# First steps of a fused token-embedding, scan and expert kernel: the taps' load and scaling moved ahead of the embedding's, the first one-hot matrix built in halves, and ten products of zeros added on TensorE

## The chip, the cores and the metric

The kernel runs on 1 core of one Trainium2 chip. The metric is the device time of one execution in microseconds (us). Before the change it was 185.24 us, the median of three runs that gave 185.24, 184.29 and 185.25. One more execution was recorded by the hardware profiler; all durations below are from that one.

## The reference

Three layers on 8 sequences of 512 token numbers, with 128 channels. Only the first is touched by the change.

```
# token layer; fake_quant(w) = round(w / s) * s, with s = max|w| / 127
e   = fake_quant(emb_weight)[x]               # 125 x 128 table, one row per token
h   = relu(e[t-1] * w[0] + e[t] * w[1])       # w = fake_quant(conv_weight), per channel, e[-1] = 0
# scan layer
u   = layernorm(h)
X_t = A X_{t-1} + B u_t                       # 4 heads of 64, each state divided by its largest entry
h   = h + (e^2 X / max|X|) C + u D
# expert layer
n   = layernorm(h); a = layernorm(n)*g + b; a = a W_attn^T + b_attn + n
h   = h + gelu((gelu(a F1_e^T + b1_e) F2_e^T + b2_e) W_next^T + b_next)
```

## The kernel before

Each of the five engines has a program of its own, written out in order by hand; semaphores join them. A batch b (0 to 7) is one sequence. Its 512 tokens are laid out so that 16 steps of 32 chunks stand side by side.

**The table.** The embedding (125x128) and the two taps (1x256, tile conv_w) are quantised on the chip. VectorE takes the largest magnitude of every row of the embedding (L634, amax_e). TensorE transposes that column against the identity matrix, which lies in the packed constants pc (L1037), so that VectorE can take the maximum over all rows (L645) and from it the scale, its inverse and the rounded table (L646 to L648). The taps are scaled in a chain of five instructions on one partition (L637 to L641): maximum, scale, reciprocal, multiply and add the rounding constant, take the constant off again. The function `chained` makes the next instruction of the engine wait for the one before it. A product with a row of ones (L1041) copies the taps to all partitions, into bank 7. Then VectorE multiplies table and taps (L653, L655), takes the combined scale scale_h (L657), and splits the products in two bf16 halves (L658); tab_ready is the semaphore behind it.

**The lookup.** It is a product with a one-hot matrix. `spread_ids(b)` (L938) copies the token numbers of batch b to 125 partitions of bank b % 2; it needs the numbers as bf16 (ids_b) and a bf16 identity (ident_b), which GpSimd casts (L413, L415) once pc and the numbers have landed. `one_hot(b)` compares them with the partition's number, 512 columns (L665) and then 31 columns (L668), the chunk before. `gather(b)` (L949) makes 16 products of 128 columns into bank 2, four for each quarter q. It waits for the one-hot matrix and, from b = 1, for bank 2 to be free. ScalarE applies scale and ReLU (L521, h).

**The loop around it.** For each batch VectorE builds the one-hot matrix two batches ahead, takes the statistics of h (L673, L677), and normalises its part of u (L697); GpSimd computes the reciprocal root (L426 to L429); ScalarE copies h, then normalises the rest of u (L538), which stands in its program ahead of the next batch's h; TensorE transposes u (L960), and in the gaps multiplies powers of A (L901) and, from batch 6, state inputs (L973). TensorE's order is fixed: `gather(b)`, `spread_ids(b + 2)`, powers, `transpose_u(b - 2)`, powers. Before the loop TensorE waits for the packed array pa and the copy pw of a part of it.

**The queues.** SyncE asks for emb_w, ids_i, pa, pw, pb, and the two expert weights, in that order. ScalarE's queue asks for pc and then conv_w. GpSimd starts with four fills (ones1, neg_half, ids_b, one column of onehot), each of which raises pool_const; ScalarE waits for the first of them ahead of a small activation that loads its table.

Behind this stage come the scan's carries, and a long stage of mixing, attention and expert products that starts at about 50 us. The change edits none of it.

Of the kernel before, what the change touches and what calls it, by code (L numbers as in the profile page):

```python
# [95 lines left out]
def build(nc, ids, emb, conv, pack_a, pack_b, pack_c, fc1, fc2, out):  # L96
    with ExitStack() as ctx:
# [3 lines left out]
        def sem(name):  # L101
            return ctx.enter_context(nc.semaphore(name))
# [64 lines left out]
        with ExitStack() as early:  # L167
            def sb_early(name, shape, dt=F32):
                return early.enter_context(nc.sbuf_tensor(name, shape, dt))


            fc2_w = sb_early("fc2_w", [P, NE * HID])
            fc1_w = sb_early("fc1_w", [P, NE * HID])
            ids_i = sb_early("ids_i", [NB, L], I32)
            ids_b = sb_early("ids_b", [P, L], BF16)
            ident_b = sb_early("ident_b", [P, P], BF16)
            centre = sb_early("centre", [P, P])
            attn_g = sb_early("attn_g", [P, CH])
        hid_p = [sb(f"hid_p{s}", [P, 2, HC, HALF], F32R) for s in range(NS)]
# [10 lines left out]
        ld_ids, ld_emb, ld_pa, ld_pb = sem("ld_ids"), sem("ld_emb"), sem("ld_pa"), sem("ld_pb")  # L190
        ld_pc, ld_fc1, ld_fc2 = sem("ld_pc"), sem("ld_fc1"), sem("ld_fc2")
        v2_ready, ld_conv = sem("v2_ready"), sem("ld_conv")
        pool_const = sem("pool_const")
        pool_link, dve_link = sem("pool_link"), sem("dve_link")
        ids_ready, amax_e_ready, tab_ready = sem("ids_ready"), sem("amax_e_ready"), sem("tab_ready")
        attn_g_ready, taps_ready = sem("attn_g_ready"), sem("taps_ready")
# [174 lines left out]
        with nc.Block() as block:  # L371

            @block.sync
            def _(sp):
                sp.dma_start(emb_w[:], emb).then_inc(ld_emb, 16)
                sp.dma_start(ids_i[:], ids).then_inc(ld_ids, 16)
                sp.dma_start(pa[:], pack_a).then_inc(ld_pa, 16)
                sp.dma_start(pw[:, 0, :], pack_a[:, PA["a"]]).then_inc(ld_pa, 16)
                sp.dma_start(pb[:], pack_b).then_inc(ld_pb, 16)
                sp.dma_start(fc2_w[:].rearrange("p (e m) -> p e m", e=NE), fc2).then_inc(ld_fc2, 16)  # L380
                sp.dma_start(fc1_w[:], fc1).then_inc(ld_fc1, 16)
                for b in range(NB - 1):

                    if b < NB - 2:
                        sp.wait_ge(res_ready, b + 1)
                    else:
                        sp.wait_ge(late_res_ready, 1)
                    sp.dma_start(out[b], res[:, b % 2, :]).then_inc(stored[b % 2], 16)
                for half in range(2):

                    b, s = NB - 1, slice(half * HALF, (half + 1) * HALF)
                    sp.wait_ge(last_res_ready, half + 1)
                    sp.dma_start(out[b][:, s], res[:, b % 2, s]).then_inc(stored[b % 2], 16)
                sp.wait_ge(stored[0], 16 * (NB // 2))
                sp.wait_ge(stored[1], 16 * (NB // 2 + 1))

            @block.gpsimd
            def _(pool):
                nc.gpsimd.memset(ones1[:], 1.0).then_inc(pool_const, 1)
                nc.gpsimd.memset(neg_half[:], -0.5).then_inc(pool_const, 1)  # L400
                nc.gpsimd.memset(ids_b[:], 0.0).then_inc(pool_const, 1)
# [76 lines left out]

            @block.scalar
            def _(act):  # L480
                act.dma_start(pc[:], pack_c).then_inc(ld_pc, 16)
                act.dma_start(conv_w[:], conv).then_inc(ld_conv, 16)
                act.wait_ge(pool_const, 1)

                nc.scalar.activation(warm[:], ones1[0:1, 0:1], ACT.Gelu)
# [30 lines left out]
                for b in range(NB + 2):  # L516
                    if b < NB:
                        act.wait_ge(gat_done, b + 1)
                        if b == 0:
                            act.wait_ge(tab_ready, 1)  # L520
                        nc.scalar.activation(h[:, b, :], bank[2][:], ACT.Relu, scale=scale_h[:]).then_inc(h_ready, 1)  # L521
                    for t in prep_tasks(b, 0):
                        copy_out_prep(t)
                    if b >= 2:
                        act.wait_ge(u_t_done, b - 1)
                        nc.scalar.activation(uT[:, b - 2, :, :].rearrange("p i k -> p (i k)"), bank[3][:],
                                             ACT.Copy).then_inc(uT_ready, 1)
                    for t in prep_tasks(b, 1):
                        copy_out_prep(t)
                    if 1 <= b <= NB and U_DVE[b - 1] < NQ:  # L530
                        act.wait_ge(rstd1_ready, b)
                        if b == 1:
                            act.wait_ge(h_ready, 1)
                        if b >= 3:
                            act.wait_ge(u_t_done, b - 2)
                        for q in range(U_DVE[b - 1], NQ):
                            s = slice(q * CH, (q + 1) * CH)
                            last = nc.scalar.activation(u[:, (b - 1) % 2, s], h[:, b - 1, s], ACT.Identity,  # L538
                                                        scale=rstd1[:, b - 1, q:q + 1], bias=shift1[:, b - 1, q:q + 1])
                        last.then_inc(u_act_ready, 1)  # L540
                    if b in (NB - 2, NB - 1):
                        copy_runs(0, b - (NB - 2))
                    if b >= NB:
                        copy_fused(b - NB)
# [78 lines left out]
            def _(dve):  # L623
                link = [0]

                def chained(ins):

                    link[0] += 1
                    ins.then_inc(dve_link, 1)
                    dve.wait_ge(dve_link, link[0])  # L630


                dve.wait_ge(ld_emb, 16)
                nc.vector.tensor_reduce(amax_e[:], emb_w[:], AX.X, ALU.max,  # L634
                                        apply_absolute_value=True).then_inc(amax_e_ready, 1)
                dve.wait_ge(ld_conv, 16)
                chained(nc.vector.tensor_reduce(amax_c[:], conv_w[:], AX.X, ALU.max, apply_absolute_value=True))  # L637
                chained(nc.vector.tensor_scalar(taps[:, 2 * CH:], amax_c[:], 1.0 / QMAX, None, ALU.mult))
                chained(nc.vector.reciprocal(inv_c[:], taps[:, 2 * CH:]))
                chained(nc.vector.tensor_scalar(taps[:, 0:2 * CH], conv_w[:], inv_c[:], ROUND, ALU.mult, ALU.add))  # L640
                nc.vector.tensor_scalar(taps[:, 0:2 * CH], taps[:, 0:2 * CH], -ROUND, None,  # L641
                                        ALU.add).then_inc(taps_ready, 1)

# [10 lines left out]
                                               op0=ALU.add, op1=ALU.mult)  # L654
                chained(nc.vector.scalar_tensor_tensor(out=tab[:, 0], in0=both, scalar=-ROUND, in1=q_taps,  # L655
                                                       op0=ALU.add, op1=ALU.mult))
                nc.vector.tensor_tensor(scale_h[:], scale_e[:], bank[7][:, 2 * CH:2 * CH + 1], ALU.mult)  # L657
                nc.vector.tensor_tensor(tab[:, 1], prod[:], tab[:, 0], ALU.subtract).then_inc(tab_ready, 1)  # L658

                def one_hot(b):  # L660
                    dve.wait_ge(idb_done, b + 1)
                    if b >= 2:
                        dve.wait_ge(gat_done, b - 1)
                    src = bank[b % 2][0:VOC, :]
                    nc.vector.tensor_scalar(onehot[:, b % 2, NCH:], src, float(VOC - 1), pc[0:VOC, PC["iota"]],  # L665
                                            ALU.min, ALU.is_equal)

                    nc.vector.tensor_scalar(onehot[:, b % 2, 1:NCH], src[:, L - NCH:L - 1], float(VOC - 1),  # L668
                                            pc[0:VOC, PC["iota"]], ALU.min, ALU.is_equal).then_inc(oh_ready, 1)

                def statistics(b, st, st_ready, mv, mv_ready):
                    for q in range(NQ):
# [4 lines left out]
                        last = nc.vector.bn_aggr(mv[:, b, q, :], st[:, b % 2, q, :])  # L677
                    last.then_inc(mv_ready, 1)

                dve.wait_ge(ld_pc, 16)  # L680
                dve.wait_ge(pool_const, 4)
                one_hot(0)
                one_hot(1)
                for b in range(NB + 1):
                    if b + 2 < NB:
                        one_hot(b + 2)
# [203 lines left out]
            def _(pe):  # L890
# [44 lines left out]
                def spread_ids(b):  # L935
                    if b >= 2:
                        pe.wait_ge(oh_ready, b - 1)
                    mm(bank[b % 2][0:VOC, :], ident_b[:, b:b + 1].broadcast_to([P, VOC]), ids_b[:], start=True,  # L938
                       stop=True).then_inc(idb_done, 1)

                def gather(b):
                    pe.wait_ge(oh_ready, b + 1)
                    if b >= 1:
                        pe.wait_ge(h_ready, b)
                    for q in range(NQ):
                        for n, (tap, part) in enumerate([(0, 0), (0, 1), (1, 0), (1, 1)]):

                            at = (q * TQ + tap) * NCH
                            last = mm(bank[2][:, q * CH:(q + 1) * CH], onehot[:, b % 2, at:at + P], tab[:, part, tap, :],  # L949
                                      start=(n == 0), stop=(n == 3))  # L950
                    last.then_inc(gat_done, 1)
# [80 lines left out]
                    mm(scan_bank(a), a1, every_run(g, a, q), start=False, stop=True).then_inc(state_done[g], 1)  # L1032


                pe.wait_ge(ld_pc, 16)
                pe.wait_ge(amax_e_ready, 1)
                nc.tensor.transpose(bank[6][:, 0:VOC], amax_e[:].broadcast_to([VOC, P]),  # L1037
# [4 lines left out]
                pe.wait_ge(ids_ready, 2)  # L1042
                spread_ids(0)
                spread_ids(1)
                pe.wait_ge(ld_pa, 32)
                for b in range(NB + 2):
                    if b == 0:
# [228 lines left out]
```

## Time and profile before

| | |
|---|---|
| runs | 185.24, 184.29, 185.25 us |
| profiled execution | 185.18 us, span 183.4 us |
| TensorE matmuls | 166.1 us busy, 91% of the span |
| VectorE | 131.8 us, 72% |
| ScalarE | 95.0 us, 52% |
| GpSimd | 92.8 us, 51% |
| mean granted TensorE clock | 0.997 |

The span is from the first to the last instruction of the trace. A row of the timeline has start, duration, engine, line, operation, tile written and tiles read, and in brackets the idle time of the engine just before it with what ended it; rows marked x16 are 16 instructions put together, with the time from the first start to the last end. PEld is the weight load of TensorE. Names with q (SPq, ACTq) are DMA issues. Line numbers such as L949 are those of the code.

### The profile page before, as it was taken

The numbers are of one execution on the slowest core, as the hardware profiler recorded it, in microseconds if no ns is written. First come the engines' busy times: TensorE is split into PE (matmuls) and PEld (weight loads), VectorE is DVE, ScalarE is ACT, GpSimd is POOL, SyncE is SP. The second block draws the span as 40 slices with busy tenths as digits, with TensorE's granted clock in tenths as the row PEclk, the third lists the DMA queues.
The fourth block names the chain that finished last, engine by engine and source line by source line (L and its number), as shares of the span: only waits on it lengthen the run. The fifth ranks groups of instructions, "written<-read, shape, count | busy, mean of one in ns | idle before, by whom it ended". The sixth has DMA issues, their size and how long they took to land.

```text
span 183.4 us, 3366 instructions
## 1 busy us (share of the span) xinstructions
PE 166.1 (91%) x1123; PEld 134.7 (73%) x1123; DVE 131.8 (72%) x405; ACT 95.0 (52%) x220; POOL 92.8 (51%) x152
## 2 busy tenths in 40 slices
PE   0599899999999898988998999999999999998993
PEld 0187685687764367865765999999998999996992
DVE  1868984494531277579996599988888898629983
ACT  3027993443223222021335683977949687686692
POOL 3107665399930000040040496695978959688700
PEclk9999999999999999999999999999999999999998
DMA  4994000000000000000000000000010100101013
GB/s 146 359 422 211 2 4 0 2 2 4 0 0 0 0 4 0 0 0 2 4 0 0 0 0 4 0 33 30 0 57 2 61 0 4 57 2 59 13 47 114
DMA packets 2325, 7.53 MB, mean 41 GB/s; under 512 B 254, under 2 KB 892, under 8 KB 2052
## 3 DMA queue, kind: packets, MB, share of 16 engines
q1 hardware_dynamic: 2162, 7.18, 10.1%
q8 instruction: 9, 0.15, 0.3%
q10 hardware_dynamic: 146, 0.13, 0.2%
q14 instruction: 8, 0.07, 0.1%
HBM read 5.22 MB, written 2.10 MB: 40 GB/s over the span
## 4 chain that ended last, share of the span: by engine, by line
PE 52%; DVE 16%; POOL 11%; issue 9%; ACT 8%; DMA 2%; POOLq 0%; DVEq 0%; ACTq 0%
PE bank L1159 7%; POOL hid_p L448 6%; PE bank L973 6%; PE bank L1026 5%; PE bank L1179 5%; PE bank L1032 5%; PE bank L1105 4%; PE bank L949 3%; PE bank L926 3%; DVE u L697 3%; PE bank L1125 2%; PE bank L1102 2%; ACT gel L572 2%; PE bank L997 2%; DVE st L673 2%
## 5 line engine op out<-in xcount | busy, mean ns | idle before, releaser
L448 POOL TENSOR_TENSOR hid_p<-hid_f,hid_p 128x256 fp32r<-128x256 f32 x52 | 37.5, 741 | 21.2 <-ACT hid_p L596 19.6
L594 ACT ACTIVATE hid_f<-bank,pa 128x256 f32<-128x256 f32 x64 | 30.9, 486 | 12.9 <-PE bank L1159 12.7
L1159 PE MATMUL bank<-xaT_p,fc_p 128*128 128x256 f32 x192 | 35.3, 295 | 1.8 <-issue 0.8
L1179 PE MATMUL bank<-hid_p,out_hi 128*128 128x256 f32 x128 | 32.2, 287 | 0.2
L467 POOL TENSOR_TENSOR rstd<-spread,neg_half 128x8 f32<-128x8 f32 x8 | 13.2, 1648 | 37.5 <-DVE spread L831 37.5
L1159 PEld LDWEIGHTS bank<-xaT_p,fc_p 128*128 128x128 f32 x192 | 26.6, 188 | 5.3 <-issue 2.1
L1179 PEld LDWEIGHTS bank<-hid_p,out_hi 128*128 128x128 f32 x128 | 23.3, 188 | 1.0 <-POOL hid_p L448 0.9
L596 ACT ACTIVATE hid_p<-bank,pa 128x256 fp32r<-128x256 f32 x48 | 23.6, 491 | 0.0
L1105 PE MATMUL bank<-pb,xh 128*128 128x128 f32 x128 | 19.5, 275 | 0.0
L512 ACT ACTIVATE X<-bank 128x512 f32<-128x512 f32 x12 | 7.2, 598 | 21.4 <-PE bank L1032 21.4
L1179 PE MATMUL bank<-hid_p,out_lo 128*128 128x256 f32 x64 | 17.8, 279 | 0.0
L673 DVE BATCH_NORM_STATS2 st<-h 128x6 f32<-128x128 f32 x64 | 13.9, 280 | 4.5 <-ACT h L521 4.2
L1105 PEld LDWEIGHTS bank<-pb,xh 128*128 128x128 f32 x128 | 16.9, 192 | 0.0
L799 DVE TRANSPOSE_TENSOR_REDUCE amax<-X 128x16 f32<-128x512 f32 x16 | 10.4, 685 | 7.4 <-ACT X L512 7.4
L780 DVE SCALAR_TENSOR_TENSOR bank<-h,ratio,bank 128x128 f32<-128x128 f32 x32 | 9.0, 350 | 5.4 <-issue 5.1
L1102 PE MATMUL bank<-pb,uT 128*128 128x128 f32 x64 | 12.5, 276 | 0.5 <-DVE xh L855 0.5
L973 PE MATMUL bank<-uT,late_b 128*128 128x512 f32 x24 | 11.6, 600 | 0.7 <-ACT X L512 0.7
L1026 PE MATMUL bank<-uT,pa 128*128 128x512 f32 x24 | 12.2, 596 | 0.0
L1032 PE MATMUL bank<-X,pa 128*128 128x512 f32 x24 | 12.1, 592 | 0.0
L1179 PEld LDWEIGHTS bank<-hid_p,out_lo 128*128 128x128 f32 x64 | 12.0, 188 | 0.0
L812 DVE SCALAR_TENSOR_TENSOR xaT_p<-bank,attn_c,xaT_p 128x256 fp32r<-128x256 f32 x16 | 7.0, 478 | 6.9 <-ACT xaT_p L610 6.9
L949 PEld LDWEIGHTS bank<-tab,onehot 125*128 125x128 bf16 x128 | 9.2, 110 | 3.7 <-issue 3.5
(127 smaller groups left out, 339.5 us busy)
## 6 DMA issues: line engine op xcount, KB each, us to landing
fc_w<-in_fc SPq DMA_DIRECT2D x2, 2048.0 KB, 12.5
out<-res SPq DMA_DIRECT2D x7, 256.0 KB, 2.0
pa<-in_pack_a SPq DMA_DIRECT2D x1, 407.0 KB, 3.4
pb<-in_pack_b SPq DMA_DIRECT2D x1, 320.0 KB, 5.8
out<-res SPq DMA_DIRECT2D x2, 128.0 KB, 1.7
pc<-in_pack_c ACTq DMA_DIRECT2D x1, 128.5 KB, 2.9
pw<-in_pack_a SPq DMA_DIRECT2D x1, 64.0 KB, 5.5
emb_w<-in_emb SPq DMA_DIRECT2D x1, 62.5 KB
```

The source lines that it names most:

```text
L448: nc.gpsimd.tensor_tensor(hid_p[1][:, half, c, :], hid_f[:, m % HID_SLOTS, :], hid_p[0][:, half, c, :].bitcast(F32), ALU.subtract).then_in ...
L594: full = nc.scalar.activation(hid_f[:, m % HID_SLOTS, :], src, ACT.Gelu, bias=bias)
L596: nc.scalar.activation(hid_p[0][:, half, c, :], src, ACT.Gelu, bias=bias).then_inc(hid_ready, 1)
L673: last = nc.vector.bn_stats(st[:, b % 2, q, :], h[:, b, q * CH:(q + 1) * CH])
L949: last = mm(bank[2][:, q * CH:(q + 1) * CH], onehot[:, b % 2, at:at + P], tab[:, part, tap, :], start=(n == 0), stop=(n == 3))
L973: last = mm(scan_bank(a), b_then(a, RUN - 1 - q), u_runs(g, q), start=(q == 0), stop=(q == RUN - 1))
L1026: mm(scan_bank(a), b_then(a, 0), u_runs(g, q), start=True, stop=False)
L1032: mm(scan_bank(a), a1, every_run(g, a, q), start=False, stop=True).then_inc(state_done[g], 1)
L1102: mm(dst, uT[:, b, q * TQ:(q + 1) * TQ, :].rearrange("p i k -> p (i k)"), pb[:, PB["d"]], start=True, stop=False)
L1105: last = mm(dst, xh[:, b % 2, a, q * P:(q + 1) * P], pb[:, PB["c"]][:, a * CH:(a + 1) * CH], start=False, stop=(a == NP - 1))
L1159: last = mm(bank[5 + n % 2][:, 0:HALF], fc1_p[w][:, e * HID + c * P:e * HID + (c + 1) * P], xaT_p[m][:, b % 2, half, :], start=(k == 0), s ...
L1179: last = mm(out_bank(b, half)[:, half * HALF:(half + 1) * HALF], out_p[w][:, e, c * CH:(c + 1) * CH], hid_p[m][:, half, c, :], start=(c == ...
```

## The change

Five edits, all in the first steps:

1. ScalarE's queue asks for conv_w first, then for pc. VectorE waits for conv_w and runs the first four instructions of the taps' chain before it waits for the embedding; the fifth comes behind the embedding's row maxima.
2. `one_hot` makes the 31 columns first; for batch 0 the 512 columns are made in two instructions of 256, and the first raises the new semaphore oh_first. `gather(0)` starts at oh_first and waits for the rest ahead of its third quarter.
3. scale_h is computed behind `one_hot(0)`, with a semaphore of its own, scale_h_ready, for which ScalarE waits in place of tab_ready.
4. GpSimd fills a new tile zeros (128x512 bf16) ahead of its other fills.
5. TensorE multiplies zeros into bank 5: six products of 512 columns before its first real instruction, and four between `spread_ids(1)` and the loop. Nothing reads the results.

```diff
@@ gpsimd
+                nc.gpsimd.memset(zeros[:], 0.0).then_inc(zeros_ready, 1)
                 nc.gpsimd.memset(ones1[:], 1.0).then_inc(pool_const, 1)
@@ scalar
+                act.dma_start(conv_w[:], conv).then_inc(ld_conv, 16)
                 act.dma_start(pc[:], pack_c).then_inc(ld_pc, 16)
-                act.dma_start(conv_w[:], conv).then_inc(ld_conv, 16)
...
                         if b == 0:
-                            act.wait_ge(tab_ready, 1)
+                            act.wait_ge(scale_h_ready, 1)
@@ vector
-                dve.wait_ge(ld_emb, 16)
-                nc.vector.tensor_reduce(amax_e[:], emb_w[:], AX.X, ALU.max,
-                                        apply_absolute_value=True).then_inc(amax_e_ready, 1)
                 dve.wait_ge(ld_conv, 16)
                 chained(nc.vector.tensor_reduce(amax_c[:], conv_w[:], AX.X, ALU.max, apply_absolute_value=True))
                 chained(nc.vector.tensor_scalar(taps[:, 2 * CH:], amax_c[:], 1.0 / QMAX, None, ALU.mult))
                 chained(nc.vector.reciprocal(inv_c[:], taps[:, 2 * CH:]))
                 chained(nc.vector.tensor_scalar(taps[:, 0:2 * CH], conv_w[:], inv_c[:], ROUND, ALU.mult, ALU.add))
+                dve.wait_ge(ld_emb, 16)
+                nc.vector.tensor_reduce(amax_e[:], emb_w[:], AX.X, ALU.max,
+                                        apply_absolute_value=True).then_inc(amax_e_ready, 1)
                 nc.vector.tensor_scalar(taps[:, 0:2 * CH], taps[:, 0:2 * CH], -ROUND, None,
                                         ALU.add).then_inc(taps_ready, 1)
...
-                nc.vector.tensor_tensor(scale_h[:], scale_e[:], bank[7][:, 2 * CH:2 * CH + 1], ALU.mult)
...
                     src = bank[b % 2][0:VOC, :]
-                    nc.vector.tensor_scalar(onehot[:, b % 2, NCH:], src, float(VOC - 1), pc[0:VOC, PC["iota"]],
+                    number = pc[0:VOC, PC["iota"]]
+                    nc.vector.tensor_scalar(onehot[:, b % 2, 1:NCH], src[:, L - NCH:L - 1], float(VOC - 1), number,
                                             ALU.min, ALU.is_equal)
-                    nc.vector.tensor_scalar(onehot[:, b % 2, 1:NCH], src[:, L - NCH:L - 1], float(VOC - 1),
-                                            pc[0:VOC, PC["iota"]], ALU.min, ALU.is_equal).then_inc(oh_ready, 1)
+                    for n0, n1 in ((0, HALF), (HALF, L)) if b == 0 else ((0, L),):
+                        last = nc.vector.tensor_scalar(onehot[:, b % 2, NCH + n0:NCH + n1], src[:, n0:n1],
+                                                       float(VOC - 1), number, ALU.min, ALU.is_equal)
+                        if n1 < L:
+                            last.then_inc(oh_first, 1)
+                    last.then_inc(oh_ready, 1)
+                dve.wait_ge(ld_pc, 16)
+                dve.wait_ge(pool_const, 4)
+                one_hot(0)
+                nc.vector.tensor_tensor(scale_h[:], scale_e[:], bank[7][:, 2 * CH:2 * CH + 1],
+                                        ALU.mult).then_inc(scale_h_ready, 1)
+                one_hot(1)
@@ tensor
                 def gather(b):
-                    pe.wait_ge(oh_ready, b + 1)
-                    if b >= 1:
+                    if b == 0:
+                        pe.wait_ge(oh_first, 1)
+                    else:
+                        pe.wait_ge(oh_ready, b + 1)
                         pe.wait_ge(h_ready, b)
                     for q in range(NQ):
+                        if b == 0 and q == NQ // 2:
+                            pe.wait_ge(oh_ready, 1)
...
+                def keep_clock(n):
+                    for _ in range(n):
+                        mm(bank[5][:], zeros[:, 0:P], zeros[:], start=True, stop=True)
+                pe.wait_ge(zeros_ready, 1)
+                keep_clock(6)
                 pe.wait_ge(ld_pc, 16)
                 pe.wait_ge(amax_e_ready, 1)
...
                 spread_ids(0)
                 spread_ids(1)
+                keep_clock(4)
                 pe.wait_ge(ld_pa, 32)
```

## Rows read from the trace of the kernel before

**Rows 1.** Busy time in 20 to 25 us: PE, PEld, DVE, ACT, POOL, clock, DMA.
```profile
20.00:25.00 5.00, 4.89 (x51) 3.99 (x50) 4.92 (x25) 4.91 (x13) 3.32 (x9) 1.00 0.01 3
```

**Rows 2.** The chain that ended last, 0 to 60 us: start, duration, what.
```profile
0.73 3.10 DMA emb_w<-in_emb
...
7.81 0.07 DVE scale_h L657
...
8.31 0.66 DVE onehot L665
8.97 0.17 DVE onehot L668
...
36.91 3.90 DVE u L697 x4
```

**Rows 3.** The timeline, 0.7 to 4.3 us.
```profile
0.73 0.39 ACTq L481 DMA_DIRECT2D pc<-in_pack_c  x1
...
0.90 0.52 POOL L401 MEMSET ids_b<- 128x512 bf16 x1
1.15 0.55 ACTq L482 DMA_DIRECT2D conv_w<-in_conv  x1
...
3.78 0.29 POOL L413 CAST ident_b<-pc 128x128 bf16<-128x128 f32 x1 [2.32 <-DMA pc<-in_pack_c]
3.85 0.29 DVE L634 TENSOR_REDUCE amax_e<-emb_w 125x1 f32<-125x128 f32 x1 [3.85 <-DMA emb_w<-in_emb]
...
4.10 0.41 DVE L637 TENSOR_REDUCE amax_c<-conv_w 1x1 f32<-1x256 f32 x1
```

**Rows 4.** DMA issues: KB each, and median us from issue to landing.
```profile
out<-res SPq DMA_DIRECT2D x2, 128.0 KB, 1.7
pc<-in_pack_c ACTq DMA_DIRECT2D x1, 128.5 KB, 2.9
pw<-in_pack_a SPq DMA_DIRECT2D x1, 64.0 KB, 5.5
```

**Rows 5.** The timeline, 4.2 to 7.5 us.
```profile
4.28 0.44 PE L1037 MATMUL bank<-pc,amax_e 125*128 125x125 f32 x1 [4.28 <-DVE amax_e L634]
...
5.28 0.28 DVE L641 TENSOR_SCALAR taps<-taps 1x256 f32<-1x256 f32 x1
5.49 0.27 DVE L645 TENSOR_REDUCE amax_all<-bank 128x1 f32<-128x125 f32 x1
...
5.71 1.19 PE L1041 MATMUL bank<-taps,ones 1*128 1x257 f32 x2 [0.98 <-DVE taps L641]
...
6.83 1.12 PE L938 MATMUL bank<-ids_b,ident_b 128*125 128x512 bf16 x2
7.02 0.42 DVE L653 SCALAR_TENSOR_TENSOR prod<-rounded,bank 125x256 f32<-125x256 f32 x1 [0.56 <-PE bank L1041]
```

**Rows 6.** The timeline, 9.2 to 18.6 us.
```profile
9.28 1.86 PE L949 MATMUL bank<-tab,onehot 125*128 125x128 bf16 x16 [1.33 <-DVE onehot L668]
...
11.61 0.75 DVE L665 TENSOR_SCALAR onehot<-bank,pc 125x512 bf16<-125x512 f32 x1 [1.66 <-PE bank L938]
...
12.06 1.86 PE L949 MATMUL bank<-tab,onehot 125*128 125x128 bf16 x16
...
13.33 0.38 DVE L677 BATCH_NORM_AGGREGATE mv<-st 128x2 f32<-128x6 f32 x4
...
14.39 0.75 DVE L665 TENSOR_SCALAR onehot<-bank,pc 125x512 bf16<-125x512 f32 x1 [0.69 <-PE bank L938]
...
14.80 1.22 PE L949 MATMUL bank<-tab,onehot 125*128 125x128 bf16 x16
...
15.79 0.88 ACT L538 ACTIVATE u<-h,shift,rstd 128x128 f32<-128x128 f32 x2 [0.70 <-POOL shift L429]
...
17.53 1.06 PE L949 MATMUL bank<-tab,onehot 125*128 125x128 bf16 x16
```

**Rows 7.** Busy time in 10 to 11 us, same columns; the clock is the third from the right.
```profile
10.00:11.00 1.00, 1.00 (x12) 1.00 (x11) 0.00 (x0) 0.00 (x0) 0.00 (x0) 1.00 0.96 410
```

More of the change, by code:

```diff
@@ L176, in build @@
             ident_b = sb_early("ident_b", [P, P], BF16)
+            zeros = sb_early("zeros", [P, L], BF16)
             centre = sb_early("centre", [P, P])
@@ L192, in build @@
         v2_ready, ld_conv = sem("v2_ready"), sem("ld_conv")
-        pool_const = sem("pool_const")
+        pool_const, zeros_ready = sem("pool_const"), sem("zeros_ready")
+        oh_first, scale_h_ready = sem("oh_first"), sem("scale_h_ready")
         pool_link, dve_link = sem("pool_link"), sem("dve_link")
@@ L678, in statistics @@
                     last.then_inc(mv_ready, 1)
[L680 to L683, printed above, removed]
                 for b in range(NB + 1):
```

## The prediction

> **What bounds the kernel now.** I read the page's first part, then the chain of waits, then the timeline of the first 20 us. TensorE is busy 91% of the span, but in the first 9 us it mostly waits: the chain begins with the embedding's load, which lands 3.1 us after its issue [rows 2], goes through VectorE's quantising, over TensorE's copy of the taps, and back to VectorE [rows 5], and reaches `gather(0)` at 9.28 us. From there to 14.39 it is on TensorE: VectorE's one-hot matrix for batch 2 is kept waiting 1.66 us, that for batch 3 another 0.69 us, both for `spread_ids` behind a gather [rows 6]. From 14.39 VectorE has a job ready at nearly each moment for some 10 us (4.92 of 5.00 us in 20 to 25, with ScalarE at 4.91 and TensorE at 4.89 beside it [rows 1]), and everything behind depends on that chain. So the reader is to watch one number: when the one-hot matrix of batch 3 starts (14.39). What is gained up to there shifts the rest.
>
> **The clock.** 16 products of a gather take 1.86 us at 9.28 and at 12.06, 1.22 us at 14.80, and 1.06 us at 17.53 [rows 6]. 15 spacings of 128 columns account for the difference: about 0.107 us each early, 0.056 us late, which are 1.2 and 2.4 GHz. The column of the granted clock says 1.00 even at 10 us [rows 7]; I go by the durations. In the gather at 14.80 some 12 of 16 are already fast ((1.86 - 1.22) / 0.051), so the clock rose near 15.2 us. TensorE had then worked without a break since 9.28, for 5.9 us; before that it had stood still for 1.33 us.
>
> **Part by part.** The sum is made against the profiled execution (185.18 us; span 183.4, 1.78 around it), which is 0.06 below the median shown (185.24).
>
> *Taps first.* conv_w is issued at 0.73 instead of 1.15. Its landing isn't in the trace; the nearest rows are 1.7 us from issue (a 128 KB store) and 2.9 us (pc) [rows 4], so it lands between 2.43 and 3.63 (that it had landed by 4.10 excludes nothing here). I take 3.0. The first four instructions of the chain need 1.14 us (about 4.14 to 5.28, [rows 3, 5]), to 4.17, past the embedding's landing at 3.85, and the row maxima 0.29: call their end R = 4.46, against 4.14 before [rows 3]; the ends of the range are 4.14 and 5.06. So this edit first costs 0.32.
>
> It gives back more. Before, the first product with real use of R was VectorE's maximum at 5.49, held by the taps' chain, and prod at 7.02, held by the copy of the taps: R + 2.88. After, the transpose starts at R + 0.14, L1041 follows at R + 0.56, takes 1.19, and prod starts 0.12 behind it, at R + 1.87 = 6.33. VectorE's own way there, from the transposed maxima (R + 0.66) through four chained steps (0.98, 5.49 to 6.47), ends at R + 1.64 and fits beside it. Net 0.69.
>
> A sentence apart: the Trainium skill, "DMA: Bandwidth & Descriptors" (Anatomy of one DMA), puts the fixed part of a DMA on the GpSimd path at about 2.0 us; if ScalarE's queue did the same, R would be near 4.16 and prod near 6.0. No row shows the landing of so small a load.
>
> *pc later.* Its issue moves from 0.73 to about 1.28 (behind 0.55 of issue). With 2.9 us it lands at 4.2. The transpose needs it at R + 0.14 = 4.6, so 0.4 covers it; GpSimd's two casts (0.29 and 0.61, the first from 3.78) then end at 5.1, ahead of `spread_ids(0)` at 6.1. If pc lands later than 4.6, each 0.1 costs 0.1. The fill of zeros (0.52, the same shape as ids_b in [rows 3]) moves the other fills by about 0.45; ScalarE is busy with issuing until 1.7 and pays nothing.
>
> *One-hot in halves, scale_h later.* From prod (7.02 [rows 5]) to the first one-hot in the chain (8.31 [rows 2]) it was 1.29, less 0.07 for scale_h: 6.33 + 1.22 = 7.55. The 31 columns cost 0.17, the half 0.40 (on the line through 0.66 for 512 columns and 0.17 for 31 [rows 2]), a semaphore 0.14 (9.14 to 9.28): oh_first frees the gather at 8.26, against 9.28. VectorE has one more instruction, 0.14 more in all; it stands before `one_hot(1)`, which then ends at about 9.4 instead of 9.95, and isn't waited for. ScalarE's wait for scale_h (8.6) ends before the gather does.
>
> *Zeros.* Six products of 512 columns at 1.2 GHz are 6 x 0.427 = 2.56 us (512 at the spacing of the slow gather rows), from 1.3 to 3.9: before R, free. The four are in the way: TensorE reaches them at R + 0.56 + 1.12 + 0.86 = 7.0 (5.71 to 6.83, two spreads) and at 1.2 GHz leaves them at 8.7, 0.45 past oh_first. So `gather(0)` starts at 8.7 and not at 8.26: 0.58 gained of 1.02. What they buy is that TensorE works without a break from about 4.6.
>
> *What the clock does.* Unbroken work for 5.9 us went before the rise; from 4.6 that gives 10.5, and with the burst from 1.3 counted whole 7.2. I take 9.0. Then three gather products are slow and 13 fast; the gather ends at 9.9, its `spread_ids(2)` lands at 10.1, and VectorE starts batch 2 at 10.15 (11.61 before), ends its one-hot matrix, statistics and averages at 12.2 (2.06 us: 11.61 to 13.71 without a gap), and goes straight on to batch 3, whose `spread_ids(3)` is there by 12.0: `gather(1)` starts at 10.75 behind h(0) and takes 1.06. 14.39 - 12.2 = 2.2 gained. With a rise at 10.5 the same walk gives 1.4, with 7.2 it gives 2.8.
>
> *What is late next.* ScalarE's h(2) stands behind u(0), which waits for GpSimd's root: the averages ended at 13.71, u(0) started at 15.79 [rows 6], 2.08 later, and takes 0.88. Counted from 12.2 this makes h(2) start at 15.1, and the statistics of batch 2 at 15.8 (17.71 before): 0.3 of the 2.2 is lost there, though h(3), which goes by batch 1, keeps 2.2. The four instructions of u at 36.91 that take 3.90 instead of about 1.1 [rows 2] run beside GpSimd's cast of fc1, which starts on the same event; I let that stay as it is. Sum: 1.9 us, 185.2 - 1.9 = **183.3 us**; by the bounds of the rise and of R, 182.5 to 184.0.
>
> **The rivals.**
>
> *Products of zeros don't raise the clock.* Nothing in the trace shows a product of zeros. Then TensorE works without break only from 8.7, the clock rises at about 14.6, and the gain is `gather(0)`'s 0.6: 184.6 us. Against it, beside: the Trainium skill, "TensorE: Matmul & The Clock Gate" (What's actually happening), says that a monitor of how busy the array has been sets the clock, which doesn't ask for the values. The page also says there that the point of the rise shifts from run to run of one kernel, which would make the median of few runs miss the forecast by tenths; the runs before (184.29 to 185.25) are as wide as that.
>
> *The clock is up before the four.* Counting the six whole, it rises at 7.2: the four then take 0.9, the gather starts at 8.26, batch 3 at about 11.6, less 0.3: 182.6 us. For it: the break between the six and the transpose is only 0.7. Against it: before, TensorE was busy for 2.2 of the 2.2 us from 5.71 with a break of 1.33 behind, and stayed slow.
>
> *conv_w lands late.* R = 5.06 takes 0.6 of the gain: 183.9.
>
> *Slower: pc becomes the first bound.* It is now issued behind conv_w and only 0.23 before the 407 KB of pa. If it is served like pw (5.5 us to landing [rows 4]) it lands at 6.8. The transpose, and behind it L1041, the spreads and the four, go with it; `gather(0)` starts at about 11.0, batch 3 at 15.0: 185.8 us. It decides from a landing of about 6.2 on, where nothing is left of the gain.
>
> **Chances.** Forecast 0.50; zeros without effect 0.17; clock up early 0.18; conv_w late 0.10; pc late 0.05. The measurement tells no change from about 0.5%, 0.93 us. Faster by more: 0.50 + 0.18 + 0.10 = 0.78. Within: 0.17 and 0.02 of the last, 0.19. Slower: 0.03. The range 182.4 to 184.8 leaves out part of the two outermost cases.
>
> **What would show it.** R (end of the row maxima) near 4.5; no idle of VectorE ahead of L653 over 0.1; `gather(0)` at 8.2 to 8.8 and some of its products at 0.056 spacing; VectorE's idle ahead of the one-hot matrices of batches 2 and 3 falling from 1.66 and 0.69 to under 0.8 and 0; the latter starting near 12.2; the stretch from there to the end as long as before. Wrong if the gathers still take 1.86 us up to 12 us, if TensorE's first transpose waits for pc, or if batch 3 starts 2 us earlier and the end doesn't.

## The result, and the profile after

The changed kernel takes 182.89 us (median of four runs, 182.64 to 183.09) against 185.24 (four runs, 184.29 to 185.25): ratio 0.9885, 95% interval 0.985 to 0.992. The profiled execution took 183.09 us with a span of 181.3, against 185.18 and 183.4: 2.09 less. The forecast was 183.3, in a range of 182.4 to 184.8. All four runs lie in that range; of the eleven later runs of the same kernel, eight don't (below).

The timeline of the changed kernel, first 15 us (start, duration, engine, line; lines are those of the changed code: L1052 are the products of zeros, L963 the gather, L669 and L672 the one-hot matrix, which now begins with its 31 columns):

```profile
0.72 0.51 ACTq L484 DMA_DIRECT2D conv_w<-in_conv  x1
...
1.26 0.37 ACTq L485 DMA_DIRECT2D pc<-in_pack_c  x1
...
1.30 2.74 PE L1052 MATMUL bank<-zeros 128*128 128x512 bf16 x6 [1.30 <-POOL zeros L401]
...
1.98 0.41 DVE L637 TENSOR_REDUCE amax_c<-conv_w 1x1 f32<-1x256 f32 x1 [1.98 <-DMA conv_w<-in_conv]
...
3.20 0.29 DVE L642 TENSOR_REDUCE amax_e<-emb_w 125x1 f32<-125x128 f32 x1
...
3.67 0.29 POOL L416 CAST ident_b<-pc 128x128 bf16<-128x128 f32 x1 [1.75 <-DMA pc<-in_pack_c]
3.83 0.41 PE L1058 MATMUL bank<-pc,amax_e 125*128 125x125 f32 x1
...
4.18 1.22 PE L1062 MATMUL bank<-taps,ones 1*128 1x257 f32 x2
...
5.52 0.42 DVE L656 SCALAR_TENSOR_TENSOR prod<-rounded,bank 125x256 f32<-125x256 f32 x1 [0.24 <-PE bank L1062]
...
6.24 1.91 PE L1052 MATMUL bank<-zeros 128*128 128x512 bf16 x4
...
7.95 1.76 PE L963 MATMUL bank<-tab,onehot 125*128 125x128 bf16 x16
...
9.96 0.25 DVE L669 TENSOR_SCALAR onehot<-bank,pc 125x31 bf16<-125x31 f32 x1 [1.41 <-PE bank L948]
...
10.63 1.05 PE L963 MATMUL bank<-tab,onehot 125*128 125x128 bf16 x16 [0.48 <-ACT h L524]
...
11.98 0.22 DVE L669 TENSOR_SCALAR onehot<-bank,pc 125x31 bf16<-125x31 f32 x1
...
14.14 0.88 ACT L541 ACTIVATE u<-h,shift,rstd 128x128 f32<-128x128 f32 x2 [1.57 <-POOL shift L432]
...
14.92 0.67 ACT L524 ACTIVATE h<-bank,scale_h 128x512 f32<-128x512 f32 x1
```

Four things stand in these rows. The taps' scaling starts 1.26 us behind the issue of their load, and the embedding's maxima start at 3.20, not at 3.85 [rows 3]. prod starts at 5.52 where it was 7.02 [rows 5]. `gather(0)` starts at 7.95, in the moment in which the four products of zeros let TensorE go, against 9.28; it is slow nearly to its end (1.76 us), and `gather(1)` is fast (1.05), so the clock rose near 9.5 us, against 15.2: the products before it go at the spacing of 1.2 GHz, those behind it at that of 2.4. The one-hot matrix of batch 3 starts at 11.98 without an idle before it, against 14.39 behind 0.69 of idle [rows 6].

The chain of waits after has the zeros in it, and the stall at u that I had left as it is:

```profile
1.30 2.74 PE bank L1052 x6
...
6.45 1.71 PE bank L1052 x4
8.15 1.55 PE bank L963 x16
...
34.81 3.92 DVE u L707 x4
```

u starts at 34.81 against 36.91 [rows 2]: 2.10 us earlier, which is the difference of the two spans. Batch 3's one-hot matrix started 2.41 earlier. So the gain is made in the first 12 us, 0.3 of it is lost again on the way to this point, and the rest is carried unchanged to the end.

### The profile page after: what moved, and what is told of

Its sections match the earlier page's. It is cut to its first block, busy times and chain, and to the rows that moved or that the text cites. A ratio compares the mean times of both kernels' runs of the same rounds, so it can differ in the third digit from the quotient of the medians.

```text
span 181.3 us, 3389 instructions
## 1 busy us (share of the span) xinstructions
PE 167.9 (93%) x1133; PEld 134.7 (74%) x1133; DVE 131.2 (72%) x406; ACT 94.4 (52%) x220; POOL 93.4 (52%) x153
## 4 chain that ended last, share of the span: by engine, by line
PE 43%; POOL 25%; issue 15%; DVE 10%; ACT 6%; POOLq 0%; ACTq 0%; DVEq 0%
POOL hid_p L451 14%; PE bank L987 6%; POOL rstd L470 5%; PE bank L1040 5%; PE bank L1046 5%; PE bank L936 3%; PE bank L1181 3%; PE bank L1201 3%; PE bank L1127 2%; PE bank L1052 2%; DVE u L707 2%; PE bank L1011 2%; PE bank L963 2%; POOL res L462 1%; PE bank L1018 1%
## 5 line engine op out<-in xcount | busy, mean ns | idle before, releaser
L1040 PE MATMUL bank<-uT,pa 128*128 128x512 f32 x24 | 12.2, 596 | 0.0
L797 DVE TENSOR_SCALAR xa<-bank,rstd,shift 128x128 f32<-128x128 f32 x32 | 10.9, 404 | 0.3
```

The source lines that it names most:

```text
L1040: mm(scan_bank(a), b_then(a, 0), u_runs(g, q), start=True, stop=False)
```

## The experiments

In all of them the time is the median of the runs, and the ratio is against the kernel before on the same chip (184.91, 184.86 and 184.89 us in the three sets).

**The changed kernel again.** It was run twice more, as the mark for the others.

> The changed kernel again, as the mark for the three runs beside it: 182.9 us, gather(0) at 7.95, clock at 2.4 GHz (by the spacing of the products) from about 9.5 us.

181.67 us, all five runs between 181.62 and 181.68; ratio 0.9829 (0.9814 to 0.9843). Not 182.9.

```profile
1.30 2.74 PE L1052 MATMUL bank<-zeros 128*128 128x512 bf16 x6 [1.30 <-POOL zeros L401]
3.83 0.41 PE L1058 MATMUL bank<-pc,amax_e 125*128 125x125 f32 x1
4.18 0.71 PE L1062 MATMUL bank<-taps,ones 1*128 1x257 f32 x2
4.82 0.64 PE L948 MATMUL bank<-ids_b,ident_b 128*125 128x512 bf16 x2
5.30 1.03 PE L1052 MATMUL bank<-zeros 128*128 128x512 bf16 x4
7.26 1.05 PE L963 MATMUL bank<-tab,onehot 125*128 125x128 bf16 x16 [0.94 <-DVE onehot L672]
```

This is the timeline of TensorE up to the first gather. Up to 3.83 every row of TensorE starts as in the execution above. Then the copy of the taps takes 0.71 and not 1.22, the two spreads 0.64 and not 1.11, the four zeros 1.03 and not 1.91: the clock had risen near 4.2 us, before any real product of size had run. The four end before 6.4, and the gather waits for the one-hot matrix, not for them.

> The changed kernel a third time, beside the three that follow. Its profiled executions so far had the clock up at about 9.5 (183.09 us) and at about 4.1 (181.65 us) with equal rows up to 4 us. If the moment differs from execution to execution, the times stand in two groups, near 181.65 and near 183; if it goes with the chip, they all fall in one.

Two groups, on one chip: 181.69, 181.73, 181.75 and 183.06, 183.27, 183.54 (median 182.41; ratio 0.9869, 0.9835 to 0.9903). With the four runs of the result and the five above, 8 of 15 executions stand at 181.62 to 181.75 and 7 at 182.64 to 183.54. I call them the early and the late group, by when the clock rises (two of the expectations below say fast and slow group). The profiled one of this set (181.75) is of the early group, with a rise near 4.9:

```profile
4.18 1.03 PE L1062 MATMUL bank<-taps,ones 1*128 1x257 f32 x2
5.14 0.64 PE L948 MATMUL bank<-ids_b,ident_b 128*125 128x512 bf16 x2
```

The moment of the rise differs by up to 5 us between the three profiled executions, and the groups are 1.4 us apart. That both occur in one set, on one chip, shows that the chip alone doesn't decide it; but the result's four runs are all late and the first repeat's five all early, so runs of one set needn't be independent, and the interval of one set doesn't cover the difference between sets. What decides the moment isn't in the profile.

**Without the products of zeros.**

```diff
-                nc.gpsimd.memset(zeros[:], 0.0).then_inc(zeros_ready, 1)
-                pe.wait_ge(zeros_ready, 1)
-                keep_clock(6)
...
-                keep_clock(4)
```

> Changed kernel without any product of zeros and without their fill. Theory A (most of the 2.35 us comes from the shorter way to the table; the zeros buy an earlier clock and pay for it with a later gather): gather(0) at about 7.35, all of its 16 products at 0.107 us, spread_ids(2) done by 9.7, gather(1) slow as well, one-hot matrix of batch 3 near 12.35 instead of 11.98: 183.3 us, 0.4 above the changed kernel. Rival B (the clock is the larger part): the clock rises 5.9 us behind the gather, at 13.2 or later, and the time is 184.0 or more.

183.19 us (182.99 to 184.54); ratio 0.9927 (0.9902 to 0.9951). Theory A's number, 183.3, is met; but the zeros are worth more than its 0.4, because the mark beside it is at 181.67: 1.5 us against the early group, 0.1 against the late one. Rival B's 184.0 or more is met by one run of six. The profiled execution was the outlier of 184.54, and it shows the rival that I had priced for the slower side. Its second gather is slow almost to its end (1.77 us from 11.78), so the clock rose near 13.3, 4.3 us behind the first gather's start at 8.99 and not 5.9:

```profile
3.17 0.28 DVE L641 TENSOR_REDUCE amax_e<-emb_w 125x1 f32<-125x128 f32 x1
...
5.34 0.47 PE L1055 MATMUL bank<-pc,amax_e 125*128 125x125 f32 x1 [5.34 <-DMA pc<-in_pack_c]
...
11.78 1.77 PE L962 MATMUL bank<-tab,onehot 125*128 125x128 bf16 x16
```

The maxima are there at 3.45 and the transpose waits for pc until 5.34, 4.1 us behind its issue at 1.25. It cost that execution 1.4 us against the others of its kernel. Single runs of other kernels with the new order of loads stand as far out (185.24 and 185.13 in one, 185.45 in another, 185.30 in a third); they weren't profiled, so that this is pc again is likely and not shown. None of the 15 executions of the changed kernel is among them.

**The six alone, the four alone.** The first kernel leaves out `keep_clock(4)`, the second `keep_clock(6)` (the wait for the fill then stands ahead of the four).

> Changed kernel without the four products of zeros ahead of the gather. gather(0) at about 7.35 instead of 7.95. If the six and the work up to 6.4 us are enough for the clock to rise at 9.5 all the same, batch 3 starts near 11.7 and the time is 182.7. If the break of 0.9 us ahead of the gather puts the rise off to past 12 us, it is as without any zeros: 183.3.

182.93 us, from 181.69 to 184.40; ratio 0.9894 (0.9854 to 0.9934). The two numbers expected, 182.7 and 183.3, lie in the middle of a spread that neither foresaw: two runs stand at 181.69 and 181.75, in the early group, and one at 184.40. The profiled one (182.74) has the time of the first expectation, but not by its way. First its TensorE timeline, then busy time by stretch (PE, PEld, DVE, ACT, POOL; the clock is the third number from the right):

```profile
4.52 0.73 PE L1062 MATMUL bank<-taps,ones 1*128 1x257 f32 x2
5.18 0.64 PE L948 MATMUL bank<-ids_b,ident_b 128*125 128x512 bf16 x2
7.57 1.47 PE L963 MATMUL bank<-tab,onehot 125*128 125x128 bf16 x16 [1.74 <-DVE onehot L672]
8.84 0.63 PE L948 MATMUL bank<-ids_b,ident_b 128*125 128x512 bf16 x1
```

```profile
6.00:8.00 2.00, 0.43 (x8) 0.46 (x9) 1.97 (x9) 0.00 (x0) 0.29 (x3) 1.00 0.94 364
8.00:10.00 2.00, 1.93 (x16) 1.57 (x14) 1.19 (x4) 0.76 (x2) 0.00 (x0) 0.51 0.94 401
10.00:12.00 2.00, 2.00 (x19) 1.93 (x19) 1.60 (x10) 0.46 (x2) 0.23 (x1) 0.64 1.02 434
```

The clock was up by the taps' copy, not at 9.5. Without the four, TensorE then stood still for 1.74 us, and in the gather behind it the clock fell: granted 0.51 in 8 to 10 us, and the spread at 8.84 takes 0.63 again. With the four the pause was 0.94 and 0.59 in two executions, and the clock stayed. So the four can hold an early rise that is otherwise lost. They aren't needed each time: the two unprofiled runs at 181.69 and 181.75 have the time of the early group without them.

> Changed kernel without the six first products of zeros, with the four. If only the unbroken work from 3.8 us on decides, the six are worth nothing: 182.9, the rise at about 9.5. If work before the break at 3.5 us counts, the rise comes 1 to 3 us later and the time is 183.3.

182.58 us (182.51 to 183.26, four runs); ratio 0.9886 (0.9867 to 0.9905). The profiled execution had some 13 fast products in a gather of 1.18 us at 7.91, a rise near 8.2. No run of it is in the group at 181.7, so the very early rise isn't seen without the six; with four runs, that the six are what brings it is likely and not shown. The late rise is no later than with them.

**The zeros alone, on the kernel before.** The fill, the six and the four are added to the kernel before, nothing else.

> Kernel before with the zeros alone (fill, six and four). gather(0) was at 9.28 and the four end at 7.95 + 1.7 = 9.65, so it starts 0.4 later; the work is unbroken from 5.7 on. Theory A: the clock rises near 10 to 11 and batch 3 starts 0.7 to 1.2 us earlier: 184.3. Rival B (clock the larger part): 183.8 or less. If zeros don't count for the clock: 185.6.

184.27 us (12 runs, 183.05 to 185.04); ratio 0.9962 (0.9944 to 0.9979): 0.6 us, the time of theory A.

```profile
9.23 1.91 PE L951 MATMUL bank<-tab,onehot 125*128 125x128 bf16 x16
...
12.07 1.29 PE L951 MATMUL bank<-tab,onehot 125*128 125x128 bf16 x16
...
13.63 0.74 DVE L667 TENSOR_SCALAR onehot<-bank,pc 125x512 bf16<-125x512 f32 x1
```

In this profiled execution (184.71) the gather starts at 9.23, where the four end, and not 0.4 later than before. The rise is near 12.5 and not at 10 to 11. Batch 3 starts 0.76 us earlier than before, inside theory A's 0.7 to 1.2.

**The loads alone, then the loads and VectorE's order.**

```diff
+                act.dma_start(conv_w[:], conv).then_inc(ld_conv, 16)
                 act.dma_start(pc[:], pack_c).then_inc(ld_pc, 16)
-                act.dma_start(conv_w[:], conv).then_inc(ld_conv, 16)
```

> Kernel before with conv_w asked for ahead of pc and nothing else. In the changed kernel the embedding's row maxima began by 3.20 us and not at 3.85. If that comes from pc being out of the embedding's way, amax_e starts at about 3.2 here too, and the transpose waits for pc at 3.6 to 3.8 instead of 4.28; as the taps' chain still stands behind it, prod comes 0.5 to 0.65 earlier: 184.7. If the earlier landing is chance of the run, amax_e stays at 3.85 and the time at 185.2.

184.24 us (12 runs, 183.97 to 185.45); ratio 0.9973 (0.9957 to 0.9989): 0.6 us. VectorE starts on the embedding at 3.22 us here:

```profile
3.22 0.28 DVE L634 TENSOR_REDUCE amax_e<-emb_w 125x1 f32<-125x128 f32 x1 [3.22 <-DMA emb_w<-in_emb]
```

With the old order of the loads VectorE waited for the embedding until 3.85 (the kernel before) and 3.70 (with the zeros alone); with the new one it was there by 3.17 to 3.33 in seven profiled executions, and in none was it seen later than that. So the early landing belongs to that order: pc, 128 KB on the other queue, no longer goes out in the same moment as the embedding. That the two loads slow each other is the likely reason; no trace shows it directly.

The way behind it isn't as expected. The transpose waits for pc until 3.94, and a step of the taps' chain takes 0.78 us in place of 0.34, for a reason I don't know; prod starts at 6.78, so of the 0.63 only 0.24 arrive there in this execution (184.88):

```profile
3.94 0.47 PE L1037 MATMUL bank<-pc,amax_e 125*128 125x125 f32 x1 [3.94 <-DMA pc<-in_pack_c]
...
4.22 0.78 DVE L640 TENSOR_SCALAR taps<-conv_w,inv_c 1x256 f32<-1x256 f32 x1
```

> Kernel before with both the order of the two loads and the order of VectorE's first instructions changed; no halves, no zeros, scale_h where it was. prod at about 5.5 instead of 7.02, gather(0) at 7.9 instead of 9.28, clock late as before. Theory A: 1.3 to 1.5 of the 2.35 us are here: 183.8. Rival B: under 0.8: 184.5 or more.

183.68 us (12 runs, 183.14 to 185.24); ratio 0.9947 (0.9925 to 0.9969): 1.2 us by the medians, and most runs between 183.4 and 183.9. The profiled execution (183.43) has prod at 5.37, `gather(0)` at 7.61, two slow gathers, and both old idles of VectorE, 1.66 and 0.69, ahead of batches 2 and 3: the front moved by 1.7 us as a block, and the clock's part is untouched.

```profile
7.61 1.86 PE L949 MATMUL bank<-tab,onehot 125*128 125x128 bf16 x16 [1.31 <-DVE onehot L668]
...
9.94 0.75 DVE L665 TENSOR_SCALAR onehot<-bank,pc 125x512 bf16<-125x512 f32 x1 [1.66 <-PE bank L938]
...
12.73 0.75 DVE L665 TENSOR_SCALAR onehot<-bank,pc 125x512 bf16<-125x512 f32 x1 [0.69 <-PE bank L938]
```

**The loads in the old order, in the changed kernel.**

> Changed kernel with the loads in the old order, pc ahead of conv_w. conv_w then lands near 2.4 (1.26 us behind its issue, as in the changed kernel) and the taps' chain ends at 3.55, ahead of the embedding at 3.85: R is 4.14 instead of 3.48, prod at about 6.1. If the early embedding is worth what it moves, 0.5 to 0.65 slower than the changed kernel beside it; in the slow group less, since gather(0) starts behind the four anyway. Rival: the order of the loads is worth nothing and VectorE's order is all: equal.

184.90 us (12 runs, 183.25 to 185.84); ratio 0.9983 (0.9954 to 1.0013): nothing is left of the gain. Neither expectation is met; it is 2.5 us slower than the changed kernel beside it, not 0.6.

```profile
1.13 0.65 ACTq L485 DMA_DIRECT2D conv_w<-in_conv  x1
...
4.16 0.41 DVE L637 TENSOR_REDUCE amax_c<-conv_w 1x1 f32<-1x256 f32 x1 [4.16 <-DMA conv_w<-in_conv]
...
5.34 0.28 DVE L642 TENSOR_REDUCE amax_e<-emb_w 125x1 f32<-125x128 f32 x1
```

The same 1 KB that landed 1.26 us behind its issue when it was first lands 3.0 us behind it when it is behind pc. VectorE waits for it until 4.16 and comes to the embedding only at 5.34, against 3.85 before. So VectorE's new order needs the new order of the loads: with the old one it turns the taps' load into the bound. This was the profiled execution, at 185.45; three of the twelve runs stand at 183.25 to 183.39, near the 0.5 to 0.65 that I had expected, and weren't profiled.

**The first one-hot matrix in one piece.**

> Changed kernel with the first one-hot matrix in one piece. The four products of zeros hold gather(0) until 7.95 and the whole matrix is ready at about 7.65 to 7.8, so the halves are worth nothing while the zeros stand there: 182.9, within 0.2. If they are worth their 0.40: 183.3.

182.93 us (181.89 to 183.37); ratio 0.9883 (0.9856 to 0.9910). By groups: 181.9 (two runs) against 181.7 of the changed kernel, and 182.8 to 183.4 against 182.6 to 183.5. The halves seem worth 0.2 where the clock is up early and the gather waits for them, and nothing that can be measured where it waits for the four.

**Two tries at a better version.** Three products of zeros ahead of the gather in place of four; and a fill of 128 columns, from which seven and four products are made.

> Changed kernel with three products of zeros ahead of the gather instead of four. Where the clock is low there they end at 7.52 and not at 7.95, so gather(0) starts 0.43 earlier: up to 0.4 off the slow group (182.6 to 182.8). Where it is already high they end before 6.0, the pause ahead of the gather grows from 0.94 to about 1.15 us; if that lets the clock fall as the pause of 1.74 did, executions near 182.7 and above take the place of those at 181.65. Forecast: slow group 182.7, fast group unchanged.

182.88 us (181.81 to 183.46); ratio 0.9882 (0.9854 to 0.9909). The profiled execution (183.31) has the gather at 7.72, in the moment the three end, its 16 products slow. Two runs are early (181.81, 182.07); the four others (182.67 to 183.46) aren't faster than the late group, against the 0.4 I had expected.

> Changed kernel with a fill of 128 columns in place of 512 (the moving operand repeats one column), and seven products first, four later. The fill takes about 0.2 and not 0.52, so TensorE starts at about 0.98 and works without a break until the same 3.9. If earlier work makes the early rise likelier, more executions stand near 181.65 and none near 183; a quarter of a microsecond less delay for pool_const changes nothing. If it doesn't, the two groups stand as in the run of the changed kernel beside it.

182.96 us (181.57 to 183.46, five runs); ratio 0.9873 (0.9840 to 0.9905). A sixth run took 185.30 and isn't counted in either. TensorE starts at 0.98 instead of 1.30; two runs stand near 181.7 (181.57, 181.81). Neither try can be told from the changed kernel beside them (182.41, 181.69 to 183.54).

## Why the prediction was right, point by point

**The sum.** 1.9 us forecast, 2.09 in the profiled execution, 2.35 by the medians. The mechanism held: the gain is made ahead of batch 3's one-hot matrix (2.41 us measured there, 2.2 forecast) and carried through. That the number came so near is in part luck, for its terms were off in both directions: `gather(0)` started 0.75 us earlier than forecast (7.95 and not 8.7), and with the clock later it took 1.76 us and not 1.2, so that batch 2 started only 0.19 earlier than forecast (9.96 and not 10.15). It is luck too that the four runs of the result all fell in the late group: 8 of 15 executions of this kernel, at 181.62 to 181.75, lie below the range of 182.4 to 184.8.

**R, the end of the maxima.** Forecast 4.46 in bounds of 4.14 to 5.06; measured 3.49. The step that failed is the landing of the two loads. conv_w took 1.26 us, outside the bounds of 1.7 to 2.9 that I had from larger transfers. (In ten profiled executions with conv_w first it took 1.25 to 1.27 six times, and 1.44, 1.68, 1.68 and 1.82; the last of these has R at 4.00.) And I held the embedding's landing fixed at 3.85 though I moved the 128 KB that went out beside it. The loads' order alone brings the embedding to 3.22. I had counted pc's move as a risk only; on the usual execution it is a gain, and pc itself lands no later than before (3.67 against 3.78 [rows 3]; 3.61 to 4.02 in nine other executions with this order, 5.34 in one). The figure of about 2.0 us for a DMA's fixed part, from the Trainium skill's "DMA: Bandwidth & Descriptors" (Anatomy of one DMA), which is for GpSimd's path, was nearer than my 2.3, but is longer than each of the ten landings of this load.

**From R to prod.** Forecast R + 1.87, measured R + 2.03. The transpose started at R + 0.34 and not at R + 0.14: the six products fill TensorE until 3.86, which with the forecast R would have cost nothing. In the kernel with the loads and VectorE in the new order and no zeros it started 0.14 behind its R of 3.52 (3.66).

**The four in the way.** Forecast to hold the gather 0.45 past oh_first; it is about 0.5. Where the four were fast, the gather started 0.61 behind the start of the first half (6.65 to 7.26); here the half starts at 6.80, which gives 7.41, and the gather starts at 7.95. `gather(0)` is 1.33 earlier than before, not 0.58: the 0.75 more is the 0.97 of R, less 0.2 lost at the transpose and here.

**The clock.** Forecast at 9.0 between 7.2 and 10.5; 9.5 in the profiled execution, and 4.2 and 4.9 in two others of the same kernel. The first was right in size. The others are beyond my range: I took the length of unbroken work ahead of the one rise of the old trace, 5.9 us, as a measure, and the same rows of TensorE up to 3.83 gave rises 5 us apart. (The 2.06 us that I took for batch 2's work is 2.10 by the rows I gave, 11.61 to 13.71; it changes nothing.) The Trainium skill's "TensorE: Matmul & The Clock Gate" says that the point shifts from run to run, and puts that at half a microsecond either way. The runs agree that it shifts and not on the size: it is up to 5 us here, 1.4 us of time, more than the tenths I allowed for it.

**Late next.** I forecast that ScalarE's h(2), behind u(0), takes back 0.3. Batch 3 gained 2.41 (11.98 against 14.39) and the end 2.1. u(0) starts at 14.14, 2.08 behind the averages as before, h(2) at 14.92 (15.1 forecast), and the statistics of batch 2 at 15.62 (15.8 forecast), so this held.

**The signs.** Of those that I had named, batch 3's start (11.98, forecast near 12.2), its idle gone to 0, some fast products in `gather(0)` and the unchanged rest held. R near 4.5 (3.49), `gather(0)` at 8.2 to 8.8 (7.95), no idle over 0.1 ahead of prod (0.24) and under 0.8 ahead of batch 2 (1.41) did not. None of the signs of a wrong forecast was seen in this execution.

**The rivals.** That zeros don't raise the clock is ruled out: it rose near 4.2 us when almost nothing but zeros had run, and no kernel without them has a run below 182.99. The early clock is real, in 8 of 15 executions by their times (two of them profiled), and at 181.65 lower than its 182.6, mostly by the same 1.0 us of R. pc as the first bound was seen once, at 5.34 and not 6.8, in a kernel without zeros, for 1.4 us. conv_w late by its price (a landing at 3.63) was seen only with the old order of the loads; in the new order the latest was 2.54.

**By parts**, from the medians: the order of the loads 0.6; with VectorE's order 1.2; with the halves and scale_h behind 1.7; with the zeros 1.8 in the late group and 3.2 in the early one. The steps stand on sets of runs up to 2.1 us wide and, where the chip is on record, on two chips, each against the kernel before beside it, so the single differences are rough.

## What to carry to other kernels

Where the first instruction waits for a load, look at the other loads that leave in the same moment, on the other queue too: here the embedding came 0.6 us sooner when 128 KB left behind it and not beside it. Ask first for what is needed first, and try the small load ahead of the large one. Idle TensorE time ahead of a chain of small products can be filled with products of zeros to get the clock up; here that paid when they ended before the real work was ready, and a pause left behind them could cost the early clock again. A change that acts on the clock makes the times fall in groups: compare group with group, and read several executions before giving it a size.

## What the runs showed of the hardware

The same kernel with the same first rows of TensorE had its clock rise from 1.2 to 2.4 GHz, by the spacing of its products, at 4.2, at 4.9 and at 9.5 us in three executions, and in time that is 181.65 and 181.75 against 183.1. A pause of 0.94 us behind an early rise left the clock up; in a kernel without the four, one of 1.74 us was followed by 0.51 granted. The column of the granted clock shows that fall, but not the low clock at the start, where it says 1.00 while products take their slow time. A load of 1 KB landed in 1.25 to 1.82 us (ten executions) when first on its queue and in 3.0 us (one execution) behind 128 KB.
